# Rows of 15 small tables found on TensorE, weights loaded behind the first gathers, channel sums by three additions

## The chip, the cores and the metric

One core of a Trainium2 chip runs the whole program. The metric is device time in microseconds (us) of one execution. Engines: PE is TensorE, DVE is VectorE, ACT is ScalarE, POOL is GpSimd, SP issues DMAs.

## The reference

39 embedding tables (widths of 1000, 1250, 12500 or 125000 rows, 16 columns) are looked up by `ids` (2048 x 39); the result `e` (2048 x 39 x 16) goes through three layers of a compressed interaction network, and its channel sums, with 16 dense columns, through a small network.

```python
def _L0_rec_ref(inputs, w0, w1, w2, b0, b1, b2):
    x0 = xk = inputs                       # (2048, 39, 16)
    direct = []
    for idx, (W, b) in enumerate([(w0, b0), (w1, b1), (w2, b2)]):
        z = jnp.einsum('bhd,bkd,hks->bsd', x0, xk, W) + b[None, :, None]
        z = jax.nn.relu(z)
        if idx != 2:
            half = z.shape[1] // 2         # 64 of 128 maps
            xk = z[:, :half, :]
            direct.append(z[:, half:, :])
        else:
            direct.append(z)
    return jnp.sum(jnp.concatenate(direct, axis=1), axis=-1)
z = _L0_rec_ref(e, L0_rec_w0, L0_rec_w1, L0_rec_w2, L0_rec_b0, L0_rec_b1, L0_rec_b2)
h = jnp.concatenate([z, dense_ctx], axis=1)
h = jnp.maximum(h @ W_top1 + b_top1, 0.0)
h = jnp.maximum(h @ W_top2 + b_top2, 0.0)
y = h @ W_top3
```

## The kernel before

The batch is cut into 16 groups of 128 rows, each into two chunks of 8 channels; a chunk has 128 rows x 8 channels = 1024 columns (`COLS`). Each of the 32 chunks is a turn of 47 tiles: tiles 0 to 19 (PAIRED) are layer 1, tiles 20 to 26 (SQUARED) are layer 0 of the next chunk, tiles 27 to 46 (LAST) are layer 2. `turns` calls every engine's `emit(turn, j)` for each tile: turns -1, 0 and 1 written out, then a hardware loop of two turns per pass, then the last turns. So the order of work on each engine's queue is fixed by hand; semaphores join them.

A tile: DVE multiplies 128 rows of products (`product`; lines 930, 945 for two tiles at once, 949), PE contracts them with a 128 x 128 weight (`contract`, line 1035). `PLAN` gives each tile a kind. F tiles are contracted in fp32, two halves of 512 columns, which the trace records as four matmuls. The others (P, V, D) are split: ACT rounds to fp32r (`high`, line 835), Pool (P, line 672) or DVE (V, D, line 904) subtracts to get `low`, and PE multiplies high by w_low, high by w_high and, two tiles later in `contract_low` (lines 1071, 1074), low by w_high: three pairs of 512-column matmuls. A V tile of 64 rows is stacked and has two pairs. A D tile's product is made in the PSUM accumulator that is free just then. Products and low parts lie in rings of `NP = 8` slots; `held` in `product` finds who used the slot last and waits for PE's count `s_mm`.

After SQUARED and PAIRED, ACT applies bias and ReLU (`take`, lines 775 to 777): two copies of the kept 64 maps to PSUM (`maps1` or `maps2`), and the other half to `direct01`. LAST's first product waits for `s_z1`, the last of the three. `channel_sum` (line 957) then reduces 8 channels to a sum of 128 x 128, at tile 28 for `direct01` (`SUM01_AT`), and for `direct2` at tile 21 of the next turn (`SUM2_AT`).

The start (turn -1): SP loads ids and weights. Pool issues one indirect DMA per field, 39 for group 0 in field order, then those of group 1. Five blocks of 8 fields (`BLOCKS`; the last has 7) are turned one by one as soon as they have landed (`turn_first`, line 1081), ACT copies a block to `x` (line 729) and writes it twice to HBM (`write_block`, line 501), and SP reads it back: the early pieces of `spread` after blocks 0 and 1 (line 572), rows of `x_thrice` and `shifted` after blocks 2, 3 and 4 (lines 483 to 494). SP takes its queue in order, and each of these needs the write to have landed. The first squares need all of `x_thrice` and `shifted`. In the start DVE also prepares weights (lines 885 to 896), behind the last gather. ACT casts `w_high` (line 734) before it copies block 0.

## Time and profile before

| | |
|---|---|
| median of 3 runs | 2479.24 us (2477.43 to 2480.89) |
| the profiled execution | 2478.53 us, span 2476.7 us |
| busy in the span | PE 96%, DVE 94%, POOL 64%, PE's weight loads 58%, ACT 44% |
| HBM | 464.57 MB read, 193 GB/s over the span |

The span runs from the first to the last instruction of the trace. A timeline row gives start, duration, engine (an added q is its queue: an instruction that issues a DMA, say), line, operation, output and inputs, how many instructions are merged, and in brackets the engine's idle time before it and what ended it. Durations of neighbours overlap a little; the distance between two starts is what an instruction holds its engine.

### The profile page before, as it was taken

To read this page: it belongs to the slowest core of one execution; us is meant where nothing else is said; L and a number is where in the kernel's file an instruction comes from. 1 tells how busy PE (TensorE), PEld (TensorE's weight loads), DVE (VectorE), ACT (ScalarE), POOL (GpSimd) and SP (SyncE) were. 2 spreads that over 40 slices of the span, in tenths; PEclk is the share of its full clock that TensorE was granted. 3 is DMA by queue.
4 is the path that set the end of the run, shared out by engine and by line. 5 is a ranking of instruction groups with operands and counts; after the bars stand their busy time and mean duration, and the time that the engine had idled before them with its cause. 6 is when DMAs were issued, how large, how long until landed. Compare 5 with 4: busy or idle time off the path is not lost.

```text
span 2476.7 us, 29974 instructions
## 1 busy us (share of the span) xinstructions
PE 2377.4 (96%) x7700; PEld 1441.3 (58%) x7700; DVE 2325.5 (94%) x1596; ACT 1099.9 (44%) x1086; POOL 1591.8 (64%) x1027
## 2 busy tenths in 40 slices
PE   0799999999999999999999999999999999999989
PEld 0455555665555666555566555566656555665556
DVE  0799999999999999999999999999999999999992
ACT  0254443454444444444444444444444444444455
POOL 7877676766767676676777667677666757543340
PEclk9999999999999999999999999999999999999999
DMA  6888887988887898888889888888988888988720
GB/s 166 203 201 197 199 197 186 218 206 196 196 204 193 205 221 200 197 196 204 193 206 221 198 197 196 204 192 214 214 196 203 192 203 193 220 212 186 195 79 11
DMA packets 176749, 477.35 MB, mean 193 GB/s; under 512 B 31216, under 2 KB 65520, under 8 KB 176448
## 3 DMA queue, kind: packets, MB, share of 16 engines
q1 hardware_dynamic: 153073, 468.91, 77.7%
q0 software_dynamic: 19968, 5.15, 2.5%
q10 hardware_dynamic: 3680, 2.95, 0.5%
q8 instruction: 13, 0.21, 0.0%
q14 instruction: 15, 0.12, 0.0%
HBM read 464.57 MB, written 12.33 MB: 193 GB/s over the span
## 4 chain that ended last, share of the span: by engine, by line
PE 75%; DVE 8%; issue 4%; POOL 2%; ACT 2%; DMA 1%; SPq 0%; DVEq 0%; POOLq 0%; ACTq 0%
PE zacc_b L1035 31%; PE zacc_a L1035 28%; PE zacc_b L1074 6%; PE zacc_a L1074 6%; DVE prod L945 4%; DVE sums L957 2%; POOL low L672 1%; DVE high L904 1%; DMA shifted<-x_periods 1%; POOL landed L650 1%; ACT direct L777 1%; ACT maps L776 1%; PE zacc_b L1071 1%; PE zacc_a L1071 1%; DVE low L904 0%
## 5 line engine op out<-in xcount | busy, mean ns | idle before, releaser
L672 POOL TENSOR_TENSOR low<-prod,high 128x1024 fp32r<-128x1024 f32 x352 | 842.2, 2397 | 586.0 <-ACT high L835 582.4
L945 DVE TENSOR_TENSOR prod<-spread,maps 128x2048 f32<-128x2048 f32 x448 | 1018.6, 2280 | 17.6 <-issue 8.2
L835 ACT ACTIVATE high<-prod 128x1024 fp32r<-128x1024 f32 (+1 forms) x576 | 607.2, 1059 | 910.1 <-DVE prod L945 486.5
L650 POOL DMA_INDIRECT landed<-in_tbl,rows_id x585 | 685.7, 1172 | 175.1 <-issue 166.7
L1035 PE MATMUL zacc_a<-prod,w_plain 128*128 128x512 f32 (+1 forms) x1472 | 679.3, 596 | 20.5 <-DVE prod L930 11.1
L1035 PE MATMUL zacc_b<-prod,w_plain 128*128 128x512 f32 (+1 forms) x1472 | 677.6, 595 | 15.3 <-DVE prod L945 15.3
L1035 PEld LDWEIGHTS zacc_a<-prod,w_plain 128*128 128x128 f32 (+1 forms) x1472 | 278.1, 190 | 287.7 <-issue 251.9
L1035 PEld LDWEIGHTS zacc_b<-prod,w_plain 128*128 128x128 f32 (+1 forms) x1472 | 277.4, 190 | 282.5 <-issue 239.1
L1074 PE MATMUL zacc_b<-low,w_high 128*128 128x512 f32 x672 | 272.0, 490 | 4.3 <-POOL low L672 4.3
L1074 PE MATMUL zacc_a<-low,w_high 128*128 128x512 f32 x672 | 271.7, 489 | 0.0
L930 DVE TENSOR_TENSOR prod<-shifted,x_thrice 128x1024 f32<-128x1024 f32 (+1 forms) x192 | 225.1, 1215 | 15.0 <-DMA shifted<-x_periods 8.9
L1035 PE MATMUL zacc_a<-high,w_low 128*128 128x512 f32 x672 | 231.7, 426 | 0.0
L1035 PE MATMUL zacc_b<-high,w_low 128*128 128x512 f32 x672 | 231.0, 425 | 0.0
L949 DVE TENSOR_TENSOR prod<-spread,maps 128x1024 f32<-128x1024 f32 (+1 forms) x192 | 229.6, 1210 | 0.0
L1035 PE MATMUL zacc_b<-high,w_high 128*128 128x512 f32 x672 | 211.3, 395 | 0.0
L1035 PE MATMUL zacc_a<-high,w_high 128*128 128x512 f32 x672 | 210.9, 395 | 0.0
L1074 PEld LDWEIGHTS zacc_b<-low,w_high 128*128 128x128 f32 x672 | 127.1, 189 | 97.0 <-issue 72.5
L1074 PEld LDWEIGHTS zacc_a<-low,w_high 128*128 128x128 f32 x672 | 127.0, 189 | 91.9 <-issue 76.6
L904 DVE TENSOR_TENSOR low<-prod,high 128x1024 fp32r<-128x1024 f32 x128 | 157.8, 1233 | 0.0
L1035 PEld LDWEIGHTS zacc_b<-high,w_low 128*128 128x128 f32 x672 | 127.0, 189 | 48.2 <-issue 19.6
L1035 PEld LDWEIGHTS zacc_a<-high,w_low 128*128 128x128 f32 x672 | 125.7, 189 | 47.5 <-issue 20.2
L1035 PEld LDWEIGHTS zacc_b<-high,w_high 128*128 128x128 f32 x672 | 127.0, 189 | 30.0
(106 smaller groups left out, 1856.3 us busy)
## 6 DMA issues: line engine op xcount, KB each, us to landing
spread<-x_periods SPq DMA_DIRECT2D x608, 512.0 KB, 9.9
shifted<-x_periods SPq DMA_DIRECT2D x188, 468.0 KB
x_thrice<-x_periods SPq DMA_DIRECT2D x93, 156.0 KB
landed<-in_tbl,rows_id POOLq DMA_INDIRECT x585, 5.2
spread<-x_periods SPq DMA_DIRECT2D x32, 256.0 KB, 21.2
x_periods<-x SPq DMA_DIRECT2D x30, 256.0 KB, 4.3
shifted<-x_periods SPq DMA_DIRECT2D x128, 44.0 KB
x_last<-x_periods SPq DMA_DIRECT2D x64, 80.0 KB
```

The lines of the kernel that those rows point to most:

```text
L650: nc.gpsimd.indirect_dma_start(out=landed[:, f, :], out_offset=None, in_=tables[f], in_offset=bass.IndirectOffsetOnAxis(ap=rows[:, f:f + 1 ...
L672: nc.gpsimd.tensor_tensor(low[0:rows, at_, :], prod[0:rows, at_, :], high[0:rows, slot(j, SPLIT, NH), :], ALU.subtract).then_inc(s_lowp, 1)
L776: nc.scalar.activation(to[HALF:128, :], z[0:HALF, :], ACT.Relu, bias=b[0:HALF, :])
L835: nc.scalar.activation(high[0:rows, h, :], made(turn, j)[0:rows, :], ACT.Copy).then_inc(s_round, 1)
L904: nc.vector.tensor_tensor(to, whole, top, ALU.subtract).then_inc(s_lowv, 1)
L930: nc.vector.tensor_tensor(to, shifted[0:rows, u % RING0, :], (x_last if u == N0 - 1 else x_thrice)[0:rows, :], ALU.mult).then_inc(s_square, 1)
L945: nc.vector.tensor_tensor(prod[:, at_:at_ + 2, :], spread[:, t:t + 2, :], maps[:, :].unsqueeze(1).to_broadcast([128, 2, COLS]), ALU.mult). ...
L949: nc.vector.tensor_tensor(to, spread[0:rows, t, :], maps[0:rows, :], ALU.mult).then_inc(s_prod, 1)
L957: nc.vector.tensor_reduce(sums[:, which, turn.odd, :], src[:, :].rearrange("p (d b) -> p b d", b=ROWS), AX.X, ALU.add).then_inc(done, 1)
L1035: return nc.tensor.matmul(z[:, hf * BANK:(hf + 1) * BANK], w, x[:, hf * BANK:(hf + 1) * BANK], start=start, stop=stop)
L1071: nc.tensor.matmul(z[:, cols], w_low[:, r, :], x[:, cols], start=False, stop=False)
L1074: done = nc.tensor.matmul(z[:, cols], w_high[0:rows, r, :], x[:, cols], start=False, stop=last)
```

## The change

Three edits. First, 15 of the 39 rows of group 0's lookup, those of the tables with 1000 and 1250 rows, are no longer gathered: the tables lie in SBUF as 125 partitions x 8 or 10 parts, DVE compares the sought numbers with row numbers (a one-hot matrix), and PE multiplies it by the table's high and low half side by side (32 columns, 8 or 10 accumulating matmuls); ACT copies the high result, DVE adds the low. Second, SP's loads are reordered: w_parted waits for block 0's gathers, w_plain, bias and small for block 1's; all_ids goes behind the weights of layer 0. ACT's cast of w_high moves behind block 2's results. Third, a channel sum is three additions at three tiles instead of one reduce; and `product` waits for ring slots at fewer places, one tile earlier where a D tile follows, and for two tiles at a time in SQUARED.

```diff
+FOUND = [{0: 8, 2: 10, 5: 8, 6: 8}, {12: 8}, {16: 8, 17: 8, 19: 8, 21: 10, 23: 10}, {25: 8, 28: 8, 31: 8}, {34: 8, 38: 8}]
+FOUND_ORDER = [f for block in FOUND for f in block]
+FOUND_ROWS, HOT, HITS, SUM_LATE, TEN_AT = 125, 4, 6, 2, 8
...
             sp.dma_start(rows_id[:, :], ids[0:ROWS, :]).then_inc(s_first, 16)
-            sp.dma_start(all_ids[:, :, :], ids.rearrange("(g p) f -> p g f", p=ROWS)).then_inc(s_all, 16)
-            sp.dma_start(ident[:, :], a["ident"]).then_inc(s_const, 16)
-            sp.dma_start(parts_in[:, 0:plan_r - PARTED0, :], a["w_parted"]).then_inc(s_parts, 16)
+            sp.dma_start(row_no, a["row_no"]).then_inc(s_row_no, 16)
+            for part in range(2):
+                some = slice(0, len(FOUND[0])) if part == 0 else slice(len(FOUND[0]), len(FOUND_ORDER))
+                sp.dma_start(sought[:, some, :], a["ids_first"][some, :].unsqueeze(0).to_broadcast(
+                    [FOUND_ROWS, some.stop - some.start, ROWS])).then_inc(s_numbers[part], 16)
+            sp.dma_start(ident[:, :], a["ident"]).then_inc(s_ident, 16)
...
+            sp.dma_start(all_ids[:, :, :], ids.rearrange("(g p) f -> p g f", p=ROWS)).then_inc(s_all, 16)
+            sp.wait_ge(s_first_g[0], 16 * (len(BLOCKS[0]) - len(FOUND[0])))
+            sp.dma_start(parts_in[:, 0:plan_r - PARTED0, :], a["w_parted"]).then_inc(s_parts, 16)
+            sp.wait_ge(s_first_g[1], 16 * (len(BLOCKS[1]) - len(FOUND[1])))
             sp.dma_start(w_plain[:, 0:plan_f - PLAIN0, :], a["w_plain"]).then_inc(s_plain, 16)
...
-                        gather(fields[0], fields[-1] + 1, s_first_g[q])
+                        for f in fields:
+                            if f not in FOUND[q]:
+                                gather(f, f + 1, s_first_g[q])
...
-            act.wait_ge(s_parts, 16)
+            for q in range(TURNED):
+                act.dma_start(table_part(table, q), table_part(a["found_rows"].rearrange("p (c d) -> p c d", d=DIM), q)
+                              ).then_inc(s_table[q], 16)
+            for q in range(TURNED):
+                act.wait_ge(s_table[q], 16)
+                nc.scalar.activation(table_part(table_hl, q)[:, :, 0:DIM], table_part(table, q), ACT.Copy).then_inc(s_table_h, 1)
             parts12 = plan_r - PARTED0
-            nc.scalar.activation(w_high[:, 0:parts12, :], parts_in[:, 0:parts12, :], ACT.Copy).then_inc(s_cast, 1)
             for q in range(TURNED):
+                for f in FOUND[q]:
+                    act.wait_ge(s_hit, FOUND_ORDER.index(f) + 1)
+                    nc.scalar.activation(landed[:, f, :], hit_of(f)[:, 0:DIM], ACT.Copy).then_inc(s_copied, 1)
+                if q == 2:
+                    act.wait_ge(s_parts, 16)
+                    nc.scalar.activation(w_high[:, 0:parts12, :], parts_in[:, 0:parts12, :], ACT.Copy).then_inc(s_cast, 1)
                 copy_block(q)
...
+            def add_found(n):
+                f = FOUND_ORDER[n]
+                dve.wait_ge(s_copied, n + 1)
+                nc.vector.tensor_tensor(landed[:, f, :], landed[:, f, :], hit_of(f)[:, DIM:2 * DIM], ALU.add
+                                        ).then_inc(s_found, 1)
...
-            dve.wait_ge(s_first_g[-1], 16 * len(BLOCKS[-1]))
+            dve.wait_ge(s_row_no, 16)
+            dve.wait_ge(s_numbers[0], 16)
+            for n, f in enumerate(FOUND_ORDER):
+                c = parts_of(f)
+                ten = TEN_AT if c == 10 else 0
+                if n == len(FOUND[0]):
+                    dve.wait_ge(s_numbers[1], 16)
+                if f == next(iter(FOUND[found_block(f)])):
+                    table_low(found_block(f))
+                if n >= HOT:
+                    dve.wait_ge(s_hit, n - HOT + 1)
+                nc.vector.tensor_tensor(hot_of(f), sought[:, n, :].unsqueeze(1).to_broadcast([FOUND_ROWS, c, ROWS]),
+                                        row_no[:, ten:ten + c].unsqueeze(2).to_broadcast([FOUND_ROWS, c, ROWS]),
+                                        ALU.is_equal).then_inc(s_hot, 1)
+                if n >= SUM_LATE:
+                    add_found(n - SUM_LATE)
+            for n in range(len(FOUND_ORDER) - SUM_LATE, len(FOUND_ORDER)):
+                add_found(n)
...
-                held = [was for was in (before(turn, i, ALL, NP) for i in range(j, j + count)) if was]
+                upto = j + count
+                if not turn.fixed and PLAN[j] == "D":
+                    upto = j
+                elif not turn.fixed and upto < TILES and PLAN[upto] == "D":
+                    upto += 1
+                elif not turn.fixed and j in SQUARED:
+                    upto = j if (j - N1) % 2 else min(j + 2, SQUARED[-1] + 1)
+                held = [was for was in (before(turn, i, ALL, NP) for i in range(j, upto)) if was]
...
-                nc.vector.tensor_reduce(sums[:, which, turn.odd, :], src[:, :].rearrange("p (d b) -> p b d", b=ROWS), AX.X,
-                                        ALU.add).then_inc(done, 1)
+                if step == 0:
+                    dve.wait_ge(ready, turn.count(1, 1))
+                    nc.vector.tensor_tensor(src[:, 0:COLS // 2], src[:, 0:COLS // 2], src[:, COLS // 2:COLS], ALU.add
+                                            ).then_inc(s_half, 1)
+                elif step == 1:
+                    dve.wait_ge(s_half, turn.count(4, 2 * which + 1))
+                    nc.vector.tensor_tensor(src[:, 0:2 * ROWS], src[:, 0:2 * ROWS], src[:, 2 * ROWS:4 * ROWS],
+                                            ALU.add).then_inc(s_half, 1)
+                else:
+                    dve.wait_ge(s_half, turn.count(4, 2 * which + 2))
...
+                    nc.vector.tensor_tensor(sums[:, which, turn.odd, :], src[:, 0:ROWS], src[:, ROWS:2 * ROWS],
+                                            ALU.add).then_inc(done, 1)
...
-                if turn.real() and j == SUM01_AT:
-                    channel_sum(turn, 0)
+                if turn.real() and 0 <= j - SUM01_AT < 3:
+                    channel_sum(turn, 0, j - SUM01_AT)
...
+            def find(f):
+                n, c = FOUND_ORDER.index(f), parts_of(f)
+                pe.wait_ge(s_table_l, found_block(f) + 1)
+                pe.wait_ge(s_hot, n + 1)
+                if n >= HITS:
+                    pe.wait_ge(s_found, n - HITS + 1)
+                for i in range(c):
+                    done = nc.tensor.matmul(hit_of(f), hot_of(f)[:, i, :], table_hl[:, in_table[f] + i, :], start=i == 0, stop=i == c - 1)
+                done.then_inc(s_hit, 1)
...
                 for q in range(TURNED):
-                    pe.wait_ge(s_first_g[q], 16 * len(BLOCKS[q]))
+                    for f in FOUND[q]:
+                        find(f)
+                    pe.wait_ge(s_first_g[q], 16 * (len(BLOCKS[q]) - len(FOUND[q])))
+                    pe.wait_ge(s_found, found(q))
```

`table_low(q)` on DVE makes a block's low table half (table minus its fp32r copy). `ids_first`, `found_rows` and `row_no` are the same inputs laid out anew.

## Rows read from the trace of the kernel before

**Rows 1.** The page, part 1: busy us, share and instructions by engine
```profile
PE 2377.4 (96%) x7700; PEld 1441.3 (58%) x7700; DVE 2325.5 (94%) x1596; ACT 1099.9 (44%) x1086; POOL 1591.8 (64%) x1027
```
**Rows 2.** Busy time by stretch: PE, PEld, DVE, ACT, POOL, granted clock, DMA share, GB/s
```profile
16.00:56.00 40.00, 1.87 (x4) 0.73 (x4) 0.00 (x0) 1.11 (x4) 30.25 (x33) 1.00 0.62 139
...
1000.00:1151.00 151.00, 150.31 (x484) 90.35 (x484) 149.18 (x105) 68.84 (x67) 105.06 (x68) 1.00 0.82 199
```
**Rows 3.** Timeline of DVE around 380, 1010 and 1155 us
```profile
382.75 2.29 DVE L945 TENSOR_TENSOR prod<-spread,maps 128x2048 f32<-128x2048 f32 x1 [3.90 <-issue]
...
1005.47 1.22 DVE L930 TENSOR_TENSOR prod<-shifted,x_last 64x1024 f32<-64x1024 f32 x1 [0.32 <-DMA shifted<-x_periods]
...
1010.16 1.92 DVE L957 TENSOR_REDUCE sums<-direct 128x128 f32<-128x1024 f32 x1
1011.99 2.28 DVE L945 TENSOR_TENSOR prod<-spread,maps 128x2048 f32<-128x2048 f32 x1
1014.19 1.22 DVE L949 TENSOR_TENSOR prod<-spread,maps 128x1024 f32<-128x1024 f32 x1
1015.32 2.28 DVE L945 TENSOR_TENSOR prod<-spread,maps 128x2048 f32<-128x2048 f32 x1
...
1155.24 1.92 DVE L957 TENSOR_REDUCE sums<-direct 128x128 f32<-128x1024 f32 x1
```
**Rows 4.** Timeline of PE at 89 us, around 1014 and 1044 us, and at 2384 us
```profile
89.22 3.75 PE L1035 MATMUL zacc_a<-prod,w_plain 128*128 128x512 f32 x4 [5.96 <-DVE prod L945]
...
1013.65 0.62 PE L1074 MATMUL zacc_b<-high,w_high 128*128 128x512 f32 x2
...
1044.27 1.88 PE L1035 MATMUL zacc_b<-prod,w_plain 128*128 128x512 f32 x4
...
1046.45 0.63 PE L1035 MATMUL zacc_b<-high,w_high 128*128 128x512 f32 x2
...
1047.38 0.63 PE L1035 MATMUL zacc_b<-high,w_low 128*128 128x512 f32 x2
...
2384.55 8.14 PE L1035 MATMUL zacc_b<-prod,w_plain 128*128 128x512 f32 x12 [5.89 <-DVE prod L945]
```
**Rows 5.** The chain that ended last, 1000 to 1160 us: start, us, what
```profile
1003.13 1.04 issue
...
1006.61 1.39 DVE prod L945
...
1008.91 1.06 DVE high L904
...
1014.33 6.34 PE zacc_a L1035 x16
...
1134.56 0.60 PE maps L1081 x5
```
**Rows 6.** Timeline of POOL, the 24th and the 39th gather
```profile
31.67 0.94 POOL L650 DMA_INDIRECT landed<-in_tbl,rows_id  x1 [0.31 <-issue]
...
50.39 0.94 POOL L650 DMA_INDIRECT landed<-in_tbl,rows_id  x1 [0.30 <-issue]
```
**Rows 7.** DMA issues of the first 120 us: last number, median us to landing
```profile
landed<-in_tbl,rows_id POOLq DMA_INDIRECT x39, 5.2
```
**Rows 8.** Timeline of ACT in the start
```profile
10.46 2.66 ACT L734 ACTIVATE w_high<-prod 128x2944 fp32r<-128x2944 f32 x1 [8.42 <-DMA prod<-in_w_parted]
...
34.58 0.28 ACT L729 ACTIVATE x<-maps 128x128 f32<-128x128 f32 x1 [2.14 <-PE maps L1081]
...
56.77 0.28 ACT L729 ACTIVATE x<-maps 112x128 f32<-112x128 f32 x1 [11.60 <-PE maps L1081]
```
**Rows 9.** Timeline of SP's queue: first and last issue for blocks 2, 3; first for 4
```profile
42.16 0.37 SPq L483 DMA_DIRECT2D x_thrice<-x_periods  x1
...
58.10 0.69 SPq L494 DMA_DIRECT2D shifted<-x_periods  x1
...
61.00 3.39 SPq L486 DMA_DIRECT2D x_thrice<-x_periods  x5
```

More of the change, by code:

```diff
@@ L138, with found, found_block, parts_of @@
 PARTED0 = N0 - PLAIN0
+def found(q):
+    return sum(len(block) for block in FOUND[:q + 1])
+def found_block(f):
+    return f // len(BLOCKS[0])
+def parts_of(f):
+    return next(block[f] for block in FOUND if f in block)
 def weight_slot(j):
@@ L179 @@
 FIRST_D = [next((j for j in of if PLAN[j] == "D"), None) for of in (PAIRED, LAST)]
+assert "D" not in (PLAN[OFFSET], PLAN[0], PLAN[LAST[0]])
 assert all(PLAN[j] != "D" or j + SUB_D <= of[-1] for of in (PAIRED, LAST) for j in of)
@@ L294, in build @@
         s_first_t = sem("s_first_t")
+        s_row_no = sem("s_row_no")
+        s_numbers = [sem(f"s_numbers{part}") for part in range(2)]
+        s_table = [sem(f"s_table{q}") for q in range(TURNED)]
+        s_table_h = sem("s_table_h")
+        s_table_l = sem("s_table_l")
+        s_hot = sem("s_hot")
+        s_hit = sem("s_hit")
+        s_copied = sem("s_copied")
+        s_found = sem("s_found")
         s_first_x = sem("s_first_x")
@@ L316, in build @@
         s_z2 = sem("s_z2")
+        s_half = sem("s_half")
         s_sum01 = sem("s_sum01")
@@ L415, in build, with table_part, hot_of, hit_of @@
         assert plan_r * MAPS <= 4 * COLS and N0 * MAPS <= COLS
+        hot_at = HOT_AT * COLS
+        sought = staged[0:FOUND_ROWS, hot_at:hot_at + len(FOUND_ORDER) * ROWS].bitcast(i32).rearrange("p (n b) -> p n b", b=ROWS)
+        hot_at += len(FOUND_ORDER) * ROWS
+        row_no = staged[0:FOUND_ROWS, hot_at:hot_at + TEN_AT + 10].bitcast(i32)
+        hot_at += TEN_AT + 10
+        parts_of_all = sum(parts_of(f) for f in FOUND_ORDER)
+        in_table = {f: sum(parts_of(g) for g in FOUND_ORDER[:n]) for n, f in enumerate(FOUND_ORDER)}
+        table = staged[0:FOUND_ROWS, hot_at:hot_at + parts_of_all * DIM].rearrange("p (c d) -> p c d", d=DIM)
+        hot_at += parts_of_all * DIM
+        table_hl = spread_r[:, :, :].rearrange("p t c -> p (t c)")[0:FOUND_ROWS, hot_at:hot_at + parts_of_all * 2 * DIM].rearrange(
+            "p (c d) -> p c d", d=2 * DIM)
+        hot_at += parts_of_all * 2 * DIM
+        hot = [spread_r[:, :, :].rearrange("p t c -> p (t c)")[0:FOUND_ROWS, hot_at + 10 * ROWS * i:hot_at + 10 * ROWS * (i + 1)]
+               for i in range(HOT)]
+        assert hot_at + 10 * ROWS * HOT <= N1 * COLS
+        def table_part(of, q):
+            first = in_table[next(iter(FOUND[q]))]
+            return of[:, first:first + sum(FOUND[q].values()), :]
+        def hot_of(f):
+            c = parts_of(f)
+            return hot[FOUND_ORDER.index(f) % HOT][:, 0:c * ROWS].rearrange("p (c b) -> p c b", b=ROWS)
+        def hit_of(f):
+            n = FOUND_ORDER.index(f) % HITS
+            return (maps1, *zacc)[n // 2][:, n % 2 * BANK:n % 2 * BANK + 2 * DIM]
         at = [0]
@@ L949, in product, with channel_sum @@
                 nc.vector.tensor_tensor(to, spread[0:rows, t, :], maps[0:rows, :], ALU.mult).then_inc(s_prod, 1)
-            def channel_sum(turn, which):
+            def channel_sum(turn, which, step):
                 src, ready, done = ((direct01, s_z1, s_sum01), (direct2, s_z2, s_sum2))[which]
-                dve.wait_ge(ready, turn.count(1, 1))
-                if not turn.odd and (not turn.fixed or turn.number() > 0):
-                    dve.wait_ge(s_feat, turn.count(1, 0))
-                nc.vector.tensor_reduce(sums[:, which, turn.odd, :], src[:, :].rearrange("p (d b) -> p b d", b=ROWS), AX.X,
-                                        ALU.add).then_inc(done, 1)
+                if step == 0:
[8 more added lines that the diff above has]
+                    dve.wait_ge(s_half, turn.count(4, 2 * which + 2))
+                    if not turn.odd and (not turn.fixed or turn.number() > 0):
+                        dve.wait_ge(s_feat, turn.count(1, 0))
+                    nc.vector.tensor_tensor(sums[:, which, turn.odd, :], src[:, 0:ROWS], src[:, ROWS:2 * ROWS],
+                                            ALU.add).then_inc(done, 1)
             def feature(turn, which):
@@ L984, in emit @@
                 sum2_at = 6 if turn.fixed and turn.number() == CHUNKS else SUM2_AT
-                if last.real() and j == sum2_at:
-                    channel_sum(last, 1)
+                if last.real() and 0 <= j - sum2_at < 3:
+                    channel_sum(last, 1, j - sum2_at)
                 if last.real() and last.odd and j == sum2_at + 3:
```

15 lines of the change are left out of this document (13 added, 2 removed).

## The prediction

> **What bounds the kernel now.** The page first [rows 1]: PE is busy 96% and DVE 94% of the span. Shares that near to each other don't say which of the two sets the time, so I read stretches [rows 2]: from 16 to 56 us neither works (PE 1.87 us, DVE nothing); in 1000 to 1151 us PE is busy 150.3 of 151 us and DVE 149.2. The change touches both stretches.
>
> *The steady part.* A turn (47 tiles) shows best by a channel sum that comes once in it: 1010.16 us, and two turns later 1155.24 [rows 3]: 145.08 us, 72.54 each. What would PE need alone? An F tile is four matmul records, a split tile three pairs, a stacked one two. From 1044.27 an F tile and one pair take until 1046.45, 2.18 us; two pairs take 0.93 from there [rows 4]: a pair is 0.465, an F tile 1.715. PLAN has 23 F, 21 split and 3 stacked tiles: 23 x 1.715 = 39.4; 69 pairs x 0.465 = 32.1; turning x, some 0.6 us every second turn, 0.3 to 0.4. Together 71.9. So PE loses about 0.65 us in a turn. Where? The chain of waits [rows 5] goes from PE's last matmul of PAIRED (1003.1) over ACT's ReLUs to DVE: product of tiles 27 and 28 (1006.61), low part of tile 26 (1008.91), then the channel sum (1010.16) and the product of tiles 29 and 30 (1011.99) [rows 3], and only then PE at 1014.33. PE's pair of 1013.65 [rows 4] was through at 1014.12, so it stood 0.2 us here; the mean of 0.65 says more in other turns. DVE's timeline [rows 3] shows why it is only just in time: each instruction starts as the one before ends; its one wait is 0.32 us, for `shifted`, before x_last's product. Its work is 72.2 us a turn, as much as the turn, and a sum that holds it 1.83 us lies between the ReLU and the product that PE wants.
>
> *The start.* Pool issues 39 gathers 1.25 us apart, the 24th at 31.67, the last at 50.39 [rows 6]; one lands after 5.2 us in the median [rows 7]. The last block is copied at 56.77 [rows 8], its loads leave SP at 61.00 [rows 9], and the first square needs them. Behind the gathers SP's queue is nearly as late: when block 2 is written (42.16) it issues for blocks 2 and 3 with no pause, the last at 58.10 for 0.69 us: 16.6 us, only 2.2 short of 61.00 [rows 9].
>
> **The change, part by part.**
>
> *Channel sums.* Out: a reduce, 1.83 us (1010.16 to 1011.99). In: additions of 512, 256 and 128 columns. 2048 columns hold DVE 2.20 us (1011.99 to 1014.19), 1024 hold it 1.13 (to 1015.32) [rows 3]; the line through both is 0.06 us + 1.04 ns a column: 0.59 + 0.33 + 0.19 = 1.11. Where an instruction follows one whose result it waits for, some more: 1008.91 to 1010.16 [rows 5, 3] is 1.25 instead of 1.13, so I add 0.12. In LAST the steps stand at tiles 28, 29 and 30, and tile 30's product is made with 29's, so step 2 follows step 1 directly; the others have a product between. Saving per turn: 2 x 0.72 - 0.12 = 1.3 us. DVE goes from 72.2 to 70.9, and PE's 71.9 becomes the bound. On the path itself only step 0 stays between the ReLU and the product of 29/30: 1.24 us earlier, more than PE's loss there. Steps 1 and 2 move behind that product; in front of tile 31's they cost 0.64, and it still starts 0.6 earlier than now. In SQUARED they come after squares 2 and 3, so the reload of `shifted` that square 2 releases gets 0.5 us more, and DVE's 0.32 goes too.
>
> Upper end: 30 turns x 0.65 = 19.5 us. Lower end: by durations instead of distances, 2.28 and 1.22 [rows 3], so 0.16 us + 1.04 ns a column, the three take 1.41, and the saving is 2 x 0.42 - 0.12 = 0.7 a turn. DVE is then at 71.5, still under PE, but with 0.4 us to spare; for that I put 12. I take 18, nearer the distances, since those are what the next instruction sees.
>
> The Trainium skill (VectorE: DVE Perf Modes, "The TRN2 errata — SBUF-src ops pay a fixed extra latency per instruction") speaks against this edit: it advises pieces of 512 elements or more, and gives an fp32 addition (N + 151)/0.96 ns. The 2.28 us of 2048 columns agrees. By it, an estimate, the three take 1.41 us; if that is also what they hold DVE, the lower end is the likely one and the sum 2461.
>
> *Merged waits for ring slots.* A product now waits also for the next tile's slot (before a D tile, and in pairs in SQUARED). The ring has 8 slots. At 1014.19 DVE starts tile 31 [rows 3], at 1014.33 PE tile 29 [rows 5]: a lead of two. A slot asked for one tile early was freed five tiles ago. Cost nothing; it would cost from a lead of six.
>
> *15 of 39 gathers.* 15 x 1.25 = 18.7 us less on Pool: the last of 24 is issued at 31.67 instead of 50.39 [rows 6] and lands at about 37.
>
> *Finding rows.* DVE compares 8 or 10 x 128 columns per field (1.13, 1.39 us): 12 x 1.13 + 3 x 1.39 = 17.7; 2016 columns of low table parts in five pieces 2.4; fifteen additions of 16 columns at about 0.15, 2.2: 22 us, in a stretch where DVE does nothing [rows 2]. PE does 126 matmuls of 32 columns, each with new weights. No such row exists. Nearest below: five 128-column transposes in 0.60 us, 0.12 each [rows 5]; above: a 512-column matmul of a pair, 0.23 [rows 4]. Both at the higher clock (2.4 GHz); after an idle stretch PE shows the lower one: four F records take 3.75 us at 89.22 against 1.88 at 1044.27 [rows 4]. The row of 16 to 56 us prints a granted clock of 1.00 [rows 2], but with five transposes in it that proves little, and I count double: 0.24 to 0.46. 32 columns are nearest to the transpose, so 0.24: 1.9 or 2.4 us a field, and 0.7 at a block's end for ACT's copy and DVE's addition. PE paces it.
> Block by block: tables (1.0 MB) and sought numbers (1.0 MB) must land, first compare at about 8 us. Block 0: 34 matmuls, turned at 17. Block 1: its eleventh gather is issued at 15.4 and lands at 21, turned at 21. Block 2: 44 matmuls, 10.6 + 1.2, turned at 33. Blocks 3 and 4: 5.8 + 0.7 and 3.9 + 0.7, at 39 and 44. The last block is 12 us earlier, not 18.7.
>
> *SP and ACT.* ACT's 2.66 us cast of w_high [rows 8] now stands between block 2's result copies and its turned block: copied at 35 (now 34.58). From a copy to SP's next issue it took 4.2 us (56.77 to 61.00) and 7.6 (34.58 to 42.16) [rows 8, 9]; I take 4.2, as the spread loads have the DMA to themselves once w_plain is in: 39. Plus SP's 16.6: block 4's loads leave at 55.7 instead of 61.00, though its data are written at 49. What is late next is SP's queue. SP waits for gathers 4 and 11 before w_parted and w_plain, so the first spread pieces leave at 23; they are needed at the first PAIRED product, after the squares, covered. DVE's preparation of weights starts after the last addition, 44, covered until 61; if not, it costs its 4 to 5 us. Gain 5.3. Bounds: a landing of 7.6 leaves 1.9; matmuls at 0.12 gain 5 more; at 0.46 block 2 comes 9 to 10 us later and block 4's loads at 65, 4 us slower. Ends: -4 to +11.
>
> *Second gathers* end 18.7 us earlier on Pool; nothing waited for them, no gain. In the end stretch PE runs eight F records at the lower clock behind the last ReLU (2384.55 [rows 4]), which covers either kind of sum: nothing.
>
> **Sum.** 2478.53 (the span and 1.8 us around it) - 18 - 5.3 = 2455. The runs' median is 0.7 above that execution. A difference under 0.2% (5 us) can't be told from none.
>
> **Rivals.**
> 1. The start gains nothing, since writes and SP's queue are as late as before: 2478.5 - 18 = 2460. For it: late weights and spread pieces share the DMA at 20 to 40 us, and a write took 7.6 once.
> 2. The steady gaps stay, because DVE's product waits for the ReLU and not for DVE's own load: only the start, 2473. Against it: from 1003.1 the ReLUs take 3.4 us, two products, a low part and step 0 another 6.4, together 9.8; PE has work for 11.2.
> 3. More than the sum: the one pause at 382.75 (DVE 3.9 us, no producer named [rows 3]) vanishes, or PE finds rows at the higher clock: 2443 to 2449.
> 4. Slower: the round trip DVE, PE, ACT, DVE of a found field doesn't overlap. Compare 1.2, 8 matmuls 3.7, copy and addition 1.1: 6 us x 15 = 90, the last block at 97, 41 us later than now; with the steady 18 off, 2501. It decides from some 4.4 us a field (mine is 2.4). Four compare buffers and six result banks speak against it.
>
> Chances: forecast 0.60 (2448 to 2462), rival 1 0.13, rival 2 0.12, rival 3 0.09, rival 4 0.06. Range 2442 to 2468: out are rival 4, most of rival 2 and the tip of rival 3. Faster: 0.60 + 0.13 + 0.09 + 0.07 of rival 2 = 0.89; same 0.05; slower 0.06.
>
> **What the profile after would show.** Three additions of about 0.69, 0.42 and 0.29 us for each reduce of 1.91; two turns in 143.8 to 144.2 us; PE without a gap before tile 29; DVE idle about 1 us a turn, on PE. Block 4 turned near 44, SP's loads for it near 56 right behind its other issues. Wrong it would be if small matmuls take over 0.4 us, if compares of integers run slower than 1.04 ns a column, or if a DVE that is earlier meets a wait for a DMA instead.

## The result, and the profile after

The changed kernel takes 2499.97 us in the median of 4 runs (2495.39 to 2501.38), the kernel before 2478.34 beside it: a ratio of 1.0083, 95% interval 1.0066 to 1.0101. It is slower by 21 us; 2455 was forecast, and 2468 was the end of the range. The profiled execution took 2495.39 us.

The page of the changed kernel, its span and part 1, against [rows 1]: the span is 16.8 us longer, PE's share goes from 96% to 97% and DVE's from 94% to 93%.

```profile
span 2493.5 us, 30349 instructions
PE 2411.6 (97%) x7826; PEld 1465.6 (59%) x7826; DVE 2310.6 (93%) x1759; ACT 1106.4 (44%) x1106; POOL 1562.0 (63%) x1012
```

**The steady part.** DVE's timeline of the changed kernel: products of x_last, which come once in a turn, 22 turns apart; then the three steps of a sum in SQUARED and the last two of one in LAST.

```profile
505.15 1.21 DVE L1045 TENSOR_TENSOR prod<-shifted,x_last 64x1024 f32<-64x1024 f32 x1
...
1008.91 0.69 DVE L1071 TENSOR_TENSOR direct<-direct 128x512 f32<-128x512 f32 x1
1009.52 1.22 DVE L1045 TENSOR_TENSOR prod<-shifted,x_thrice 128x1024 f32<-128x1024 f32 x1
1010.65 0.41 DVE L1075 TENSOR_TENSOR direct<-direct 128x256 f32<-128x256 f32 x1
1010.99 1.22 DVE L1045 TENSOR_TENSOR prod<-shifted,x_thrice 128x1024 f32<-128x1024 f32 x1
1012.12 0.28 DVE L1082 TENSOR_TENSOR sums<-direct 128x128 f32<-128x128 f32 x1
1012.32 1.22 DVE L1045 TENSOR_TENSOR prod<-shifted,x_thrice 117x1024 f32<-117x1024 f32 x1
...
1095.15 0.42 DVE L1075 TENSOR_TENSOR direct<-direct 128x256 f32<-128x256 f32 x1
1095.61 0.29 DVE L1082 TENSOR_TENSOR sums<-direct 128x128 f32<-128x128 f32 x1
...
2113.50 1.21 DVE L1045 TENSOR_TENSOR prod<-shifted,x_last 64x1024 f32<-64x1024 f32 x1
```

A turn is (2113.50 - 505.15)/22 = 73.11 us; the same two products stood at 497.42 and 2093.71 in the kernel before, 72.56. Yet the additions hold DVE exactly as worked out: 0.61, 0.34 and 0.20 us by the distances of the starts (forecast 0.59, 0.33, 0.19), and 0.46 for the second where the third follows it directly (0.33 + 0.12). So the sums save what they should, and something else takes more. DVE's list of waits, 200 to 2350 us (us in total, times, longest):

```profile
DVE prod L1060 <- issue: 47.9, 31, 3.3
DVE prod L1045 <- DMA shifted<-x_periods: 16.0, 24, 1.4
```

In the kernel before these were 8.2 us (16 times) and 10.3. 28 of the 31 stops, 43.2 us, stand at one place, some 50 us behind the product of x_last. DVE and then PE there in one turn of the changed kernel:

```profile
1135.45 1.22 DVE L1064 TENSOR_TENSOR zacc_b<-spread,maps 128x1024 f32<-128x1024 f32 x1
1138.10 2.29 DVE L1060 TENSOR_TENSOR prod<-spread,maps 128x2048 f32<-128x2048 f32 x1 [1.43 <-issue]
1140.31 1.22 DVE L1012 TENSOR_TENSOR low<-zacc_b,high 128x1024 fp32r<-128x1024 f32 x1
1141.56 1.23 DVE L1064 TENSOR_TENSOR zacc_b<-spread,maps 128x1024 f32<-128x1024 f32 x1
```

```profile
1135.67 1.88 PE L1160 MATMUL zacc_a<-prod,w_plain 128*128 128x512 f32 x4
1136.98 1.02 PE L1199 MATMUL zacc_a<-low,w_high 128*128 128x512 f32 x2
1137.85 0.64 PE L1160 MATMUL zacc_a<-high,w_low 128*128 128x512 f32 x2
```

The product at 1138.10 is that of tiles 13 and 14, a D tile before it (12, into the accumulator at 1135.45) and one behind it (15, at 1141.56). It begins 0.10 us after PE's low-part pair of 1136.98 has ended (1138.00). The bracket says "issue", no producer: a wait for a ring slot is a count of PE's matmuls.

**The start.** PE, ACT and SP's queue of the changed kernel, against [rows 8, 9]:

```profile
20.23 4.02 PE L1217 MATMUL maps<-spread_r 125*128 125x32 f32 x18 [20.23 <-DMA ident<-in_ident]
...
29.71 0.45 PE L1206 MATMUL maps<-ident,landed 128*128 128x128 f32 x1 [1.69 <-DVE landed L967]
```

```profile
44.59 0.27 ACT L797 ACTIVATE x<-maps 128x128 f32<-128x128 f32 x1
```

```profile
52.80 0.32 SPq L542 DMA_DIRECT2D x_thrice<-x_periods  x1
...
67.75 0.69 SPq L553 DMA_DIRECT2D shifted<-x_periods  x1
68.48 3.38 SPq L545 DMA_DIRECT2D x_thrice<-x_periods  x5
```

Block 0 is turned at 29.71 instead of 16.29; block 2 is copied at 44.59 instead of 34.58, and block 2's loads leave SP at 52.80 instead of 42.16. Block 4 is copied at 53.89, 2.9 us sooner than before, for nothing: its loads stand behind 15.7 us of SP's issues and leave at 68.48, 7.5 us later than before. What held the first small matmul is `ident`, a 64 KB load issued at 2.34. Issues of the first 30 us (KB, us to landing) and busy time by stretch (the last two numbers: DMA share, GB/s):

```profile
all_ids<-in_ids SPq DMA_DIRECT2D x1, 312.0 KB, 20.5
ident<-in_ident SPq DMA_DIRECT2D x1, 64.0 KB, 17.8
```

```profile
12.00:16.00 4.00, 0.00 (x0) 0.00 (x0) 4.00 (x4) 0.00 (x0) 3.11 (x3) 1.00 0.38 130
16.00:20.00 4.00, 0.00 (x0) 0.00 (x0) 0.04 (x1) 0.79 (x1) 3.06 (x4) 1.00 0.37 129
```

While PE waits for a load, the 16 DMA engines are busy 0.38 of the time. That is some 6 of 16, while `all_ids`, issued at 4.85, takes 20.5 us to land. In the trace each of the loads over 125 partitions raises its semaphore once at its issue and five times as data land. `ident` has 128 partitions, and of the 16 rises of its semaphore 11 come from 4.3 to 5.9 us, the last five from 19.9 to 20.2: it waited for five of the engines only. The Trainium skill (DMA: Bandwidth & Descriptors, "Why a DMA increments its semaphore by 16 and not by 1") says why: a DMA issued by SP or ACT is spread over the largest number of engines up to 16 that divides its slowest dimension, and takes the lowest-numbered ones. For 125 that is 5. The five rises agree, and the runs over 128 partitions below test it.

### The profile page after: what moved, and what is told of

It is laid out like the page before. It is cut to its first block, busy times and chain, and to the rows that moved or that the text cites. A ratio compares the mean times of both kernels' runs of the same rounds, so it can differ in the third digit from the quotient of the medians.

```text
span 2493.5 us, 30349 instructions
## 1 busy us (share of the span) xinstructions
PE 2411.6 (97%) x7826; PEld 1465.6 (59%) x7826; DVE 2310.6 (93%) x1759; ACT 1106.4 (44%) x1106; POOL 1562.0 (63%) x1012
## 4 chain that ended last, share of the span: by engine, by line
PE 70%; DVE 9%; issue 7%; DMA 6%; POOL 4%; SPq 2%; ACT 1%; DVEq 0%; ACTq 0%; POOLq 0%
PE zacc_a L1160 29%; PE zacc_b L1160 26%; PE zacc_a L1199 6%; DMA shifted<-x_periods 5%; PE zacc_b L1199 5%; DVE prod L1060 3%; POOL low L738 2%; DVE low L1012 2%; DVE prod L1045 2%; POOL landed L716 2%; DVE prod L1064 1%; DMA spread<-in_found_rows 1%; PE zacc_a L1196 1%; PE zacc_b L1196 1%; SPq L615 0%
## 5 line engine op out<-in xcount | busy, mean ns | idle before, releaser
L716 POOL DMA_INDIRECT landed<-in_tbl,rows_id x570 | 658.4, 1155 | 175.3 <-issue 160.2
L1045 DVE TENSOR_TENSOR prod<-shifted,x_thrice 128x1024 f32<-128x1024 f32 (+1 forms) x192 | 230.7, 1215 | 37.6 <-DMA shifted<-x_periods 21.1
```

The source lines that it names most:

```text
L716: nc.gpsimd.indirect_dma_start(out=landed[:, f, :], out_offset=None, in_=tables[f], in_offset=bass.IndirectOffsetOnAxis(ap=rows[:, f:f + 1 ...
L1045: nc.vector.tensor_tensor(to, shifted[0:rows, u % RING0, :], (x_last if u == N0 - 1 else x_thrice)[0:rows, :], ALU.mult).then_inc(s_square, 1)
```

## The experiments

Four groups of four, each beside its own runs of the kernel before: 2490.71 and 2489.03 us in groups 1 and 4, 2477.62 and 2477.80 in groups 2 and 3. Ratios are to those, and are compared within a group where tenths of a per cent matter: between groups the kernel before itself differs by 13 us.

### Group 1: undo one edit, or make one alone

The old waits in the changed kernel:

```diff
-                upto = j + count
-                if not turn.fixed and PLAN[j] == "D":
-                    upto = j
-                elif not turn.fixed and upto < TILES and PLAN[upto] == "D":
-                    upto += 1
-                elif not turn.fixed and j in SQUARED:
-                    upto = j if (j - N1) % 2 else min(j + 2, SQUARED[-1] + 1)
-                held = [was for was in (before(turn, i, ALL, NP) for i in range(j, upto)) if was]
+                held = [was for was in (before(turn, i, ALL, NP) for i in range(j, j + count)) if was]
```

> The changed kernel with the ring-slot waits of the kernel before. If the merged waits stop DVE in the middle of PAIRED (one idle stretch of about 1.5 us per turn, before the product of tiles 13 and 14) and this is what made the steady part slower: the idle stretch goes, a turn falls from 72.9 to about 71.9, and the time is about 2468 (start still 7 late). If instead the earlier sums only push DVE into its waits for DMA: the turn stays near 72.9 and the time near 2497.

Measured: 2473.87 us, 0.9927 (0.9905 to 0.9948), turns of 71.97 us: the first of the two expectations. The other two edits together are a gain; the merged waits turn it into a loss. In the profiled execution the start is some 11 us later than in the changed kernel's (first square on PE at 86.68 instead of 75.33), so the ratio says little on the start.

The kernel before with the three-step sums alone (`channel_sum(turn, which, step)` and its calls, as in the change):

> The kernel before with only the three-step channel sums. If the sums are worth what the prediction says: 18 us faster than before, 2460, DVE idle over 1 us a turn. If the gaps of PE are not due to DVE's load: within 5 us of before. If three additions cost more than a reduce: slower.

Measured: 2617.12 us, 1.0505 (1.0490 to 1.0521). Slower, as the third expectation has it, but not for its reason. DVE of this kernel:

```profile
560.74 2.29 DVE L946 TENSOR_TENSOR prod<-spread,maps 128x2048 f32<-128x2048 f32 x1 [7.56 <-issue]
...
568.54 2.29 DVE L946 TENSOR_TENSOR prod<-spread,maps 128x2048 f32<-128x2048 f32 x1 [4.38 <-issue]
```

This pair of stops comes once in a pass of the loop (every second turn). The queue rows of 420 to 2180 us (packets, MB) show what else is there only in this kernel:

```profile
q14 instruction: 55, 0.45, 0.1%
```

The kernel before the change, the changed one and the padded one below have no such packet in that window; here they come at 557.0, 558.0 and 566.2 us, 155 us later again, five a pass: parts of a program are fetched anew in each pass. That was a new question, for group 3.

The kernel before with the merged waits alone (the diff above, reversed):

> The kernel before with only the merged ring-slot waits. If the merged waits make DVE stop and DVE has no slack to make up for it: 30 turns x up to 1.5 us, 25 to 45 us slower. If the slot was always free by then (lead of two tiles): no change, within 5 us.

Measured: 2547.82 us, 1.0226 (1.0212 to 1.0239). Turns of 74.6 us, and the same stop, in one turn 1.74 us before the product of tiles 13 and 14. 28 of its stops stand there. That is 57 us, more than the 25 to 45 expected: a turn is 2.09 us longer than before, for a stop of 1.7. Here DVE is the bound with nothing to spare, and each microsecond that it stands is lost; in the changed kernel the shorter sums hide part of it (1.1 us a turn, 73.11 against 71.97 with the old waits).

The kernel before with found rows and late weights alone:

> The kernel before with only the start changed (rows found on PE, late weights). If the start alone explains its part: first square at about 74 instead of 66.5 us, 6 to 8 us slower in all, steady part as before (72.5 a turn). If the start's other effects (code, buffers, Pool earlier) touch the steady part: more than 10 slower.

Measured: 2496.30 us, 1.0011 (0.9996 to 1.0027): no gain in the start, and turns of 72.60 us, as before. Its twelve runs lie from 2485.04 to 2507.48, and the profile is of the slowest: ACT stands there for 11.0 us once, block 2 is copied at 68.92, and the first square on PE comes at 95.59 (74 expected). What the start costs by itself can't be read from this kernel.

### Group 2: which half of the waits, and the loads over 128 partitions

The tables, sought and row numbers with three rows of padding:

```diff
-            sp.dma_start(row_no, a["row_no"]).then_inc(s_row_no, 16)
+            sp.dma_start(row_no_all, a["row_no"]).then_inc(s_row_no, 16)
...
-                sp.dma_start(sought[:, some, :], a["ids_first"][some, :].unsqueeze(0).to_broadcast(
-                    [FOUND_ROWS, some.stop - some.start, ROWS])).then_inc(s_numbers[part], 16)
+                sp.dma_start(sought_all[:, some, :], a["ids_first"][some, :].unsqueeze(0).to_broadcast(
+                    [ROWS, some.stop - some.start, ROWS])).then_inc(s_numbers[part], 16)
...
-                act.dma_start(table_part(table, q), table_part(a["found_rows"].rearrange("p (c d) -> p c d", d=DIM), q)
+                act.dma_start(table_part(table_all, q), table_part(a["found_rows"].rearrange("p (c d) -> p c d", d=DIM), q)
```

> The changed kernel with one edit: the loads of the tables, the sought numbers and the row numbers go over 128 partitions instead of 125 (three rows of padding). Theory A (these loads run through 5 of the core's 16 DMA engines, and everything else that is loaded in the first 25 us stands behind them): ident lands near 8 us instead of 20, the first small matmul starts at 8 to 10 us instead of 20.2, the spread begins some 8 to 12 us sooner, and the time against the kernel before falls from 1.0083 to about 1.003 to 1.005 (8 to 12 us of 2480). Rival B (the amount of data, not the number of engines, sets the landing): the first small matmul stays at 17 to 20 us, ratio 1.007 to 1.010.

Measured: 2494.93 us, 1.0061 (1.0047 to 1.0074).

```profile
8.00:12.00 4.00, 0.00 (x0) 0.00 (x0) 2.37 (x3) 0.79 (x1) 3.09 (x4) 1.00 1.06 380
12.00:16.00 4.00, 2.77 (x13) 2.77 (x14) 2.65 (x4) 1.13 (x3) 3.39 (x3) 1.00 0.84 179
```

The DMA share goes from 0.38 to 0.84 in 12 to 16 us, the first small matmul from 20.23 to 13.23, the last block is turned at 45.8 instead of 53.4, and the first square on PE comes at 68.9 instead of 75.3: theory A on the landing, though `ident` lands at 13.2 and not near 8. The time gains 0.2% (0.3% beside waits_d of this group), half of what A said.

The same with the old waits:

> The changed kernel with the old waits for ring slots and the 128-partition loads: found rows and three-step sums stay. Theory A (waits and loads are two separate losses): 0.9927 from the undone waits alone, less 8 to 12 us of start: 0.988 to 0.990 of the kernel before, about 2452 us where that takes 2480. Rival B (the start is not on the path once the waits are undone, since its time varies more from run to run than the loads explain): 0.992 to 0.994.

Measured: 2464.42 us, 0.9944 (0.9930 to 0.9957), above both expectations. They started from group 1's 0.9927, whose kernel before took 13 us longer. Beside the kernels with harmless waits and 125 partitions in groups 2 and 3 (0.9958 and 0.9955, below) the loads are worth 0.1%, which the intervals can't tell from nothing.

Only the half that belongs to D tiles:

```diff
-                elif not turn.fixed and j in SQUARED:
-                    upto = j if (j - N1) % 2 else min(j + 2, SQUARED[-1] + 1)
```

> The changed kernel with only the half of the merged waits that belongs to tiles of kind D (a D tile's product asks for nothing, the product before it asks for two slots); the products of SQUARED wait one by one as before. Theory A (the stop of 1.4 to 1.5 us a turn before the product ahead of tile 15, a D tile, is what costs, and it belongs to this half): all of the loss stays, ratio 1.006 to 1.009, DVE idle about 2.3 us a turn. Rival B (the loss is in the pairs of SQUARED, which are followed by the spread of tile 27 that PE reaches late): ratio 0.993 to 0.995.

Measured: 2499.88 us, 1.0090 (1.0075 to 1.0105), the whole loss. DVE stops 30 times for 46.7 us, 28 times at the same product.

Only the half of SQUARED:

```diff
-                if not turn.fixed and PLAN[j] == "D":
-                    upto = j
-                elif not turn.fixed and upto < TILES and PLAN[upto] == "D":
-                    upto += 1
-                elif not turn.fixed and j in SQUARED:
+                if not turn.fixed and j in SQUARED and PLAN[j] != "D" and not (upto < TILES and PLAN[upto] == "D"):
                     upto = j if (j - N1) % 2 else min(j + 2, SQUARED[-1] + 1)
```

> The changed kernel with only the half of the merged waits that belongs to SQUARED (one wait for two products); D tiles and the products before them wait as before. Theory A: ratio 0.993 to 0.995, as with all old waits, since the stop before the product ahead of tile 15 is gone; at most the gap of 0.4 us before tile 27 stays, 0.5 per cent of a turn. Rival B: 1.006 to 1.009. If both halves cost, each ends between, near 1.000.

Measured: 2467.76 us, 0.9958 (0.9944 to 0.9972). No loss there.

### Group 3: one wait, the program's place, the order of ident

Only tile 15's wait is undone:

```diff
-                if not turn.fixed and PLAN[j] == "D":
+                if not turn.fixed and PLAN[j] == "D" and j != 15:
                     upto = j
-                elif not turn.fixed and upto < TILES and PLAN[upto] == "D":
+                elif not turn.fixed and upto < TILES and PLAN[upto] == "D" and upto != 15:
                     upto += 1
```

> The changed kernel in which only tile 15's wait is no longer merged: the product of tiles 13 and 14 asks for its own two slots, tile 15's product for its own. The other D tiles and the pairs of SQUARED stay merged. Theory A (the whole loss is the stop before the product of 13 and 14, 31 times, 47.9 us, because slot 15 was last read by tile 7, whose low part PE reads two places later, so that DVE may be only four places ahead of PE there): ratio 0.995 to 0.997 against the kernel before, the same as with only the SQUARED half, turns of 71.9 us. Rival B (the stop moves to the products ahead of tiles 12, 40 and 43, which are merged in the same way): ratio 1.003 to 1.009, turns of 72.6 or more with a stop of over 1 us at another product.

Measured: 2467.34 us, 0.9955 (0.9942 to 0.9969). DVE's waits of this kernel, 200 to 2350 us:

```profile
DVE prod L1045 <- DMA shifted<-x_periods: 20.0, 29, 1.4
DVE prod L1060 <- issue: 12.6, 17, 3.6
```

Theory A. One wait of 47 tiles is the whole loss: from 0.9955 to 1.0083 is 1.3%, 32 us, and within group 2 the two halves differ by as much (0.9958, 1.0090). Of the 17 stops marked "issue" that are left, 16 stand before the product of tiles 2 and 3.

The kernel before with three-step sums and the SQUARED half of the waits:

> The kernel before with the three-step sums and the SQUARED half of the merged waits; no found rows. It issues fewer waits on DVE than the three-step sums alone, which stopped once in two turns for 12.5 us with 68 packets on the instruction queue. Theory A (the engine's program is fetched again in each pass of the loop when the loop's code grows past what is kept, or falls unluckily): with fewer instructions in the loop 6 or 7 packets again, ratio 0.992 to 0.995 (71.9 instead of 72.55 us a turn, 30 turns). Rival B (the SQUARED half frees too little): the stop stays, ratio 1.04 to 1.05. Rival C (the stop has another cause than code): 68 packets and no stop, or a stop and 6 packets.

Measured: 2460.59 us, 0.9922 (0.9908 to 0.9936), no instruction packet in 420 to 2180 us.

The kernel before with three-step sums, and instructions ahead of DVE's loop:

```diff
-            nc.vector.memset(sums[:, :, :, :], 0.0)
+            for n in range(40):
+                nc.vector.memset(sums[:, 0, 0, n:n + 1], 0.0)
+            nc.vector.memset(sums[:, 0, 0, 40:], 0.0)
+            nc.vector.memset(sums[:, 0, 1, :], 0.0)
+            nc.vector.memset(sums[:, 1, :, :], 0.0)
```

> The kernel before with the three-step sums, and DVE's first memset cut into 43 pieces, 42 instructions more ahead of the loop and none in it, about 3 us of a DVE that is idle there. Theory A (where the loop lies in the engine's program decides whether it is fetched again): the stop of 12.5 us in two turns goes, 6 or 7 packets, ratio 0.992 to 0.996. Rival B (the size of the loop decides): the stop stays, 68 packets, ratio 1.048 to 1.053.

Measured: 2461.30 us, 0.9922 (0.9908 to 0.9935). The loop is the one that took 2617 us, word for word; with 42 instructions in front of it the ratio is 5.8% lower, some 144 us (the two kernels were not run side by side). Its products of x_last at 494.86 and 2077.38 lie 22 turns apart: 71.93 us a turn, against 77.46 without the 42 instructions. So where the loop lies decides, not its size alone. The Trainium skill (Runtime: NRT & Kernel Launch, "Instruction fetch mechanics") gives a mechanism: most engines keep two blocks of 16 KB, 256 instructions each, and a jump to code outside them waits for a fetch. By it a loop that fits in two blocks at one place touches three at another. The packets at the stops agree in kind, though they are of 8 KB; that they are DVE's, and that its loop lies across three blocks here, was not read from the program itself.

The changed kernel with old waits and 128 partitions, and ident first:

```diff
+            sp.dma_start(ident[:, :], a["ident"]).then_inc(s_ident, 16)
             sp.dma_start(row_no_all, a["row_no"]).then_inc(s_row_no, 16)
...
-            sp.dma_start(ident[:, :], a["ident"]).then_inc(s_ident, 16)
```

> The changed kernel with old waits and 128-partition loads, and ident loaded ahead of the sought numbers instead of behind them. Theory A (with loads over 16 engines the first small matmul waits for ident alone, 13.2 us against compares ready at 10.9): first small matmul at about 11 to 11.5, block 0 turned 2 us sooner, the first spread pieces leave SP 2 us sooner; time 0 to 2 us less than without that, ratio 0.993 to 0.9945. Rival B (the SP queue behind block 2 is the bound of the start and block 2's landing is set by the spread pieces beside it): first matmul sooner, first square unchanged within 1 us, ratio 0.994 to 0.995.

Measured: 2456.81 us, 0.9910 (0.9894 to 0.9925), better than expected. PE's rows:

```profile
11.00 3.99 PE L1213 MATMUL maps<-spread_r 125*128 125x32 f32 x18 [11.00 <-DVE spread_r L987]
...
46.61 0.43 PE L1202 MATMUL maps<-ident,landed 128*112 128x128 f32 x1 [0.52 <-issue]
...
66.97 8.62 PE L1156 MATMUL zacc_a<-prod,w_plain 128*128 128x512 f32 x16 [19.92 <-DVE prod L1041]
```

The last block is turned at 46.61, and its loads leave at 59.75 because SP issues without a pause from 43.78: 16.0 us. Block 2 was copied at 34.96, as forecast, and SP's next issue came 8.8 us later.

### Group 4: the start by itself, and controls

The old-waits kernel with ident first, but 125 partitions:

> The changed kernel with old waits and ident loaded ahead of the sought numbers; the loads stay over 125 partitions (5 DMA engines). Theory A (ident behind the sought numbers on the 5 shared engines is what made the first small matmul late; the number of engines matters only through it): first small matmul at 13 us, set by the first compare (11.6 + 1.2), most of the gain of the combined edit (from 0.9955 to 0.991) is here: 0.991 to 0.993. Rival B (the few engines also hold up tables, x's writes and the spread): first small matmul at 13, but blocks 1 and 2 turned later and the first square 3 us or more behind the 66.97 of the combined edit: 0.993 to 0.9955.

Measured: 2466.57 us, 0.9918 (0.9889 to 0.9947); first small matmul at 17.54 (13 in both theories), first square on PE at 75.5. The interval spans both ratios; the profile decides for rival B: the order alone brings neither blocks nor square forward.

The kernel before with the mended start alone:

> The kernel before with found rows and late weights alone (one reduce, old waits), loads over 128 partitions and ident first. The start by itself: its first square came at 66.97 in the kernel with three-step sums against 67.85 before, and the pause near 380 us was shorter there. Theory A (the start is worth what its first square shows, about 1 us): ratio 0.998 to 1.000. Rival B (the start as predicted, 5 us, once its loads are in order): 0.9975 to 0.9985. Theory C (the gain of 7 us that the combined kernel had at 420 us comes from the pause alone, which depends on where the code lies): 1.000 with a pause as long as before, 0.997 with a short one.

Measured: 2477.20 us, 0.9954 (0.9940 to 0.9967): 11.5 us, more than any theory said. First square on PE at 66.94, where the padded kernel before has it at 77.86 in this group (67.85 in the kernel before's own trace). SP's queue of the padded kernel before, against [rows 9]:

```profile
41.06 0.37 SPq L483 DMA_DIRECT2D x_thrice<-x_periods  x1
...
69.53 0.70 SPq L494 DMA_DIRECT2D shifted<-x_periods  x1
70.93 6.67 SPq L486 DMA_DIRECT2D x_thrice<-x_periods  x5
```

The issues for blocks 2 and 3 begin 1.1 us sooner than in [rows 9] and take 28.5 us instead of 15.9; so they do in the kernel with the merged waits alone (41.07 to 70.07, group 1). In this kernel they take 15.1 (42.62 to 57.73). So most of the 11.5 us is a slow start of the kernel before in this group, which the mended start does not show; the time in us is that of the kernel before in groups 2 and 3.

All that the runs favour (three-step sums, mended start, SQUARED half):

> All that the runs so far favour: three-step sums, found rows over 128 partitions with ident first, and of the merged waits only the SQUARED half. Sums 0.9922, start another 0.001, the SQUARED half nothing: 0.990 to 0.992, about 2455 us where the kernel before takes 2478. If the SQUARED half gains by itself (fewer waits on DVE): 0.989.

Measured: 2460.66 us, 0.9905 (0.9874 to 0.9935). Its seven runs fall into 2456.7 to 2460.7 and 2479.8 to 2481.6; the profile is of the second kind, and its ACT stops in the start:

```profile
47.32 0.82 ACTq L563 DMA_DIRECT2D x_periods<-x  x2
64.27 0.18 ACT L813 ACTIVATE landed<-zacc_b 128x16 f32<-128x16 f32 x1 [16.98 <-remote]
```

The kernel before with the 42 instructions and nothing else:

> The kernel before with the same 42 instructions more ahead of DVE's loop and nothing else, the control of the padded sums. If the instructions only move the program: ratio 0.999 to 1.001, turns of 72.55. If padding gains by itself (a shorter pause at the loop's first pass), up to 0.2 per cent: 0.998. If this program now falls where it is fetched again in each pass: a stop of over 10 us in two turns and 1.04 or more.

Measured: 2490.34 us, 1.0005 (0.9996 to 1.0014). Padding by itself does nothing here.

## Why the prediction was wrong

**The step that failed** is "Merged waits for ring slots": "A slot asked for one tile early was freed five tiles ago. Cost nothing; it would cost from a lead of six." The lead of two was read at tiles 29 to 31, behind the ReLU, where PE has just caught up with DVE; it was taken for the whole turn. And the five was not worked out for each tile. By the kernel's own slot function, the products of tiles 13 and 14 ask for the slots of tiles 5 and 6, both F: PE must be through with place 6, so DVE may lead by 7. Tile 15's slot was last tile 7's, a P tile whose low part PE reads two places later (`LATE = 2`): with the merged wait PE must be through with place 9, and the lead may be 4. The profile shows it: in the turn above the product starts 0.10 us behind the end of a low-part pair. The other merged D tiles (8, 12, 37, 40, 43) and the pairs of SQUARED leave a lead of 5 or more, and cost nothing that groups 2 and 3 could measure. Undoing one wait removes 32 us.

The kernel before had shown it. In its trace these are the product of tiles 2 and 3, that of tiles 13 and 14, and the pair in which PE reads tile 7's low part:

```profile
1040.49 4.49 DVE L945 TENSOR_TENSOR prod<-spread,maps 128x2048 f32<-128x2048 f32 x2 [0.21 <-issue]
...
1054.95 2.28 DVE L945 TENSOR_TENSOR prod<-spread,maps 128x2048 f32<-128x2048 f32 x1
...
1055.85 1.02 PE L1074 MATMUL zacc_b<-low,w_high 128*128 128x512 f32 x2
```

DVE starts the product of 13 and 14 when PE is through with tile 8 and at work on 9: a lead of 5, counted as above, where the merged wait allows 4. (Counted so, the prediction's lead of two at tile 31 is 3.) The pair ends 1.92 us after that start (1056.87). A wait for its end, with the 0.10 us seen above, costs 2.0 us a turn; with the merged waits alone a turn is 2.09 us longer. And of the 16 stops marked "issue" in that kernel 15 (4.3 us) stand before the product of tiles 2 and 3, the one place where its own waits allow a lead of only 4.

**The second miss** is "first compare at about 8 us" and what hangs on it. It came at 12.3 (the numbers landed at 11.6), and the first small matmul at 20.2, since ident, which the transposes and these matmuls wait for, shared five DMA engines with 2 MB. Most steps behind it were right: small matmuls 0.21 us apart (18 in 4.02 us; 0.24 to 0.46 was counted), compares 1.22 us, additions 0.17, the round trip of a field overlapped (rival 4 did not happen), and what was late next was SP's queue, for 15.7 us (52.80 to 68.48; forecast 16.6). One more term was too small: from block 2's copy to SP's next issue 4.2 us were put, and it took 8.2 (44.59 to 52.80), and 8.8 with the loads mended. With block 2 on time (34.96) block 4's loads then leave at 59.75, 1.2 us sooner than before and not 5.3. With three-step sums on both sides, from 0.9922 without to 0.9955 with found rows is 8 us lost, where a gain of 5.3 was forecast and the bound was a loss of 4. With the loads mended it is 0.9910, a gain of 3 us that the intervals can't tell from none; the 11.5 us of group 4 are mostly the kernel before's slow start there.

**The sums** were right in mechanism and size: 0.9922, 19.3 us for a forecast 18; turns of 71.93 for a computed load of PE of 71.9. The distances, not the durations, are what the additions hold DVE: 0.61, 0.34 and 0.20 us. The Trainium skill (VectorE: DVE Perf Modes, "The TRN2 errata — SBUF-src ops pay a fixed extra latency per instruction") gives the durations (0.69, 0.42 and 0.29 by its formula; the trace has 0.69, 0.41 and 0.28), but the next instruction starts some 0.08 us before they end.

**The sum again, with measured terms:** sums -19.3, start +8, one wait +32: +21 us, and +21 were measured. By its number rival 4 (2501) came nearest, by luck: the round trip that it counts did overlap, and the last block was turned at 53.4, not 97. By its mechanism rival 1 (the start gains nothing) was the nearest, and too mild. Rival 3's pause was still there (3.26 us). No rival had a wait for a slot in it. The last of its signs of being wrong, "a DVE that is earlier meets a wait for a DMA instead", is there: waits for `shifted` are 20.0 us in the kernel without the bad wait, 10.3 before; they are covered, since its turns (72.0 us) are PE's load.

**Open:** why SP issues the same loads in 28.5 us instead of 15.9 in some starts with 39 gathers (seen in one profile each of groups 1 and 4, whose kernels before take 11 to 13 us longer; groups 1 and 3 ran on the same chip, so it is not the chip), and what stops ACT for 17 us in some starts (no instruction packet lies in 49 to 75 us there).

## What to carry to other kernels

A wait that asks for two things is as late as the later one, so before merging work out for every place how far ahead it lets the waiting engine run, with the last reader of each slot, and compare with the lead that the trace shows at that place, not with the lead at another. Give a load a partition count that 16 divides, above all when small urgent loads follow it on the queue. When a loop gets a few instructions longer and the time jumps by per cents, look for instruction packets in the middle of the run before blaming the edit.

## What was not expected of the hardware

- The kernel with the same DVE loop took 2617 or 2461 us, depending on 42 instructions in front of it: stops of 7.56 and 4.38 us in every second turn, with five 8 KB instruction packets in each pass.
- In such a stop PE stood 6.7 us. The granted clock is then 0.50 in 564 to 569 us, the lower level (1.2 GHz), and 1.00 (2.4 GHz) in 580 to 600.
- Loads over 125 partitions left the DMA engines 0.38 busy while a 64 KB load took 17.8 us; over 128 partitions the share was 0.84 to 1.06, and the same load landed at 13.2 us.
- SP issued the same loads of blocks 2 and 3 in 15.9 or 28.5 us, in executions of kernels that differ in their start by 42 small DVE instructions or by nothing.
